# A rope block computed once: the product with the sine swaps the two halves of 64 rows

## The reference

```python
q_hk  = (hidden_q @ Wq.T).reshape(B, S, 16, 128)
q_big = jnp.einsum('bshk,hkq->bshq', q_hk, w_kc_q)      # 384 wide
q_big = q_big * cos + rotate_half(q_big) * sin          # rope over the 384
q_r   = jnp.einsum('bshq,hqr->bhsr', q_big, W_qr)       # 64 wide
# rotate_half(x) = concatenate([-x[..., 192:], x[..., :192]])
attn  = softmax(q_r . k_r);  ctx_c = attn @ kv_r
```

## Time and profile before

| what | value |
| --- | --- |
| runs of the kernel | 1120.31, 1122.6 and 1126.47 us, median 1122.6 us |
| the profiled execution | 1126.12 us |
| its span, first to last instruction | 1124.3 us |
| mean granted TensorE clock | 0.966 |
| PE busy in the span | 992.5 us, 88% |
| DVE busy | 693.1 us, 62% |
| ACT, POOL busy | 540.8 us, 513.3 us |

### The profile page before, as it was taken

One profiled execution on the slowest core, in us unless ns is written; L12 is line 12 of the kernel. 1 busy time (PEld: TensorE's weight loads), 2 busy tenths in 40 slices (PEclk: granted clock), 3 DMA queues, 4 the chain that ended last, 5 costly groups with the idle time before them and its releaser, 6 DMA issues. The chain is left out here.

```text
span 1124.3 us, 19812 instructions
## 1 busy us (share of the span) xinstructions
PE 992.5 (88%) x6202; PEld 578.6 (51%) x6202; DVE 693.1 (62%) x1187; ACT 540.8 (48%) x1224; POOL 513.3 (46%) x646
## 2 busy tenths in 40 slices
PE   0679999999999999899658569999999988998998
PEld 0335555555555555444223235777777764444543
DVE  2768778787878777396678534766666663323112
ACT  1345656565655656200376415777777773105400
POOL 2956766667666766100133205666666671110000
PEclk9999999999999999999888869999999999998999
DMA  7111121303122101341300002222222003204001
GB/s 219 43 57 58 51 66 42 89 28 89 31 86 65 42 19 30 140 160 65 112 1 29 20 19 67 66 66 65 65 65 65 0 1 143 73 1 159 0 29 38
DMA packets 24191, 69.23 MB, mean 62 GB/s; under 512 B 3162, under 2 KB 5338, under 8 KB 21719
## 3 DMA queue, kind: packets, MB, share of 16 engines
q1 hardware_dynamic: 18656, 58.01, 15.4%
q10 hardware_dynamic: 5492, 10.67, 3.6%
HBM read 64.99 MB, written 3.67 MB: 61 GB/s over the span
## 5 line engine op out<-in xcount | busy, mean ns | idle before, releaser
L1077 POOL TENSOR_SCALAR scratch<-scratch,rinv 112x375 f32<-112x375 f32 x256 | 155.4, 620 | 148.8 <-DVE rinv L944 148.8
L819 ACT ACTIVATE scratch<-ps,mxn 112x375 f32<-112x375 f32 x256 | 144.1, 571 | 59.0 <-DVE mxn L939 58.9
L1194 PE MATMUL ps<-arena 128*128 128x512 f16 x672 | 149.5, 385 | 2.3 <-PEq L600 2.3
L939 DVE TENSOR_REDUCE mxn<-ps 112x2 f32<-112x750 f32 x128 | 119.5, 933 | 41.7 <-PE ps L633 41.7
L1059 POOL TENSOR_TENSOR scratch<-scratch 128x896 f32<-128x896 f32 x64 | 104.5, 1633 | 60.1 <-DVE scratch L963 59.6
L684 PE MATMUL ps<-xnT,scratch 128*128 128x448 f16 x576 | 125.1, 364 | 3.8 <-DVE scratch L1014 2.4
L671 PE MATMUL ps<-scratch,kvn_hi 125*128 125x224 f16 x768 | 119.9, 260 | 4.4 <-DVE scratch L985 2.3
L656 PEld LDWEIGHTS ps<-ident,scratch 112*125 112x125 f32 x768 | 100.0, 188 | 42.4 <-issue 35.3
L1069 POOL TENSOR_TENSOR scratch<-scratch 128x375 f16<-128x375 f32 x128 | 115.3, 901 | 10.9
L656 PE MATMUL ps<-ident,scratch 112*125 112x112 f32 x768 | 106.5, 275 | 10.9 <-DVE scratch L1005 9.1
L829 ACT ACTIVATE scratch<-ps 125x672 f16<-125x672 f32 x128 | 94.2, 736 | 43.5 <-PE ps L656 42.5
(11 more groups left out here) (137 smaller groups left out, 1440.0 us busy)
## 6 DMA issues: line engine op xcount, KB each, us to landing
scratch<-in_wq SPq DMA_DIRECT2D x16, 512.0 KB, 5.0
scratch<-in_wo SPq DMA_DIRECT2D x16, 512.0 KB, 3.6
wabs<-in_w ACTq DMA_DIRECT2D x32, 256.0 KB, 3.0
scratch<-in_w SPq DMA_DIRECT2D x8, 1024.0 KB, 4.8
scratch<-in_W SPq DMA_DIRECT2D x8, 1024.0 KB, 6.4
scratch<-in_kcq SPq DMA_DIRECT2D x8, 512.0 KB, 5.5
scratch<-in_qr SPq DMA_DIRECT2D x32, 128.0 KB, 3.8
scratch<-in_kcq SPq DMA_DIRECT2D x8, 384.0 KB, 3.5
```

Of the source, the lines that this page charges most:

```text
L819: last = nc.scalar.activation(prob[0:S, s % 2, hh, :], scores_ps[0:S, hh, 0:L], ACT.Exp, bias=mxn[0:S, s % 2, hh:hh + 1], accum_out=rsum[0 ...
L939: nc.vector.tensor_reduce(mxn[0:S, s % 2, :], scores_ps[0:S, :, 0:L], AX_X, ALU.max, negate=True).then_inc(max_done, 1)
L1077: last = nc.gpsimd.tensor_scalar(prob[0:S, s % 2, hh, :], prob[0:S, s % 2, hh, :], rinv[0:S, s % 2, hh:hh + 1], P_SCALE, ALU.mult, ALU.mult)
L1194: last = nc.tensor.matmul(ps[:, b, :], a[:, h, ds(t * P, P)], c[:, h, :], start=(h == 0 and i == 0), stop=(h == H - 1 and i == 2))
```

## The change

The fourth block is gone: (B, u, 3) is taken out of all lists, and the split of the weight takes 2 x 384 of its 2 x 512 elements. The product of block 2 with the sine is made from the bank of block 2 by two operations of 64 rows each: one reads rows 64 to 127 and writes rows 0 to 63, the other the other way round. The sine table of block 2 is loaded with its halves exchanged, so that bank and table are read at the same rows; its load is three transfers in place of one. The second addition on POOL and the reuse of roped and turned wait for (B, u, 2) in place of (B, u, 3). The banks are dealt out again over 38 groups in place of 42.

```diff
-    [TURN, SCORES, ("A", 3), ("S", 1), ("K", 3), *ropes(2, 2, 3)],
-    [TURN, SCORES, *ropes(3, 0, 1), ("S", 2), ("K", 4), *ropes(3, 2, 3)],
+    [TURN, SCORES, ("A", 3), ("S", 1), ("K", 3), *ropes(2, 2)],
+    [TURN, SCORES, *ropes(3, 0, 1), ("S", 2), ("K", 4), *ropes(3, 2)],
...
-        kcq_hi, a = view(scratch, a, [2, 512], F16)
-        kcq_lo, a = view(scratch, a, [2, 512], F16)
+        kcq_hi, a = view(scratch, a, [2, DCQ], F16)
+        kcq_lo, a = view(scratch, a, [2, DCQ], F16)
...
-            act.dma_start(ropeq[:, :, :], tab["ropeq"]).then_inc(s_ropeq, 16)
+            act.dma_start(ropeq[:, 0:5, :], tab["ropeq"][:, 0:5, :]).then_inc(s_ropeq, 16)
+            act.dma_start(ropeq[0:R, 5, :], tab["ropeq"][R:P, 5, :]).then_inc(s_ropeq, 16)
+            act.dma_start(ropeq[R:P, 5, :], tab["ropeq"][0:R, 5, :]).then_inc(s_ropeq, 16)
...
-                        for dst, t in (((roped[:, u % 2, 0], 0), (turned[:, 1], 4)),
-                                       ((roped[:, u % 2, 1], 1), (turned[:, 0], 3)),
-                                       ((roped[:, u % 2, 2], 2),),
-                                       ((turned[:, 2], 5),))[j]:
+                        low, high, every = slice(0, R), slice(R, P), slice(0, P)
+                        for dst, t, rows, to in (
+                                ((roped[:, u % 2, 0], 0, every, every), (turned[:, 1], 4, every, every)),
+                                ((roped[:, u % 2, 1], 1, every, every), (turned[:, 0], 3, every, every)),
+                                ((roped[:, u % 2, 2], 2, every, every), (turned[:, 2], 5, high, low),
+                                 (turned[:, 2], 5, low, high)))[j]:
+                            n_rows = rows.stop - rows.start
                             last = nc.vector.tensor_tensor(
-                                dst.rearrange("p (b n) -> p b n", b=B // 2), src,
-                                ropeq[:, t:t + 1, :].to_broadcast([P, B // 2, S]), ALU.mult)
+                                dst[to].rearrange("p (b n) -> p b n", b=B // 2), src[rows],
+                                ropeq[rows, t:t + 1, :].to_broadcast([n_rows, B // 2, S]),
+                                ALU.mult)
...
-                        pool.wait_ge(group_out, nth_group(q, ("B", u, 3 if second else 1)))
+                        pool.wait_ge(group_out, nth_group(q, ("B", u, 2 if second else 1)))
```

More of the change, by code:

```diff
@@ L70 @@
     [TURN, SCORES, ("A", 2), ("S", 0), ("K", 2), *ropes(2, 0, 1)],
-    [TURN, SCORES, ("A", 3), ("S", 1), ("K", 3), *ropes(2, 2, 3)],
-    [TURN, SCORES, *ropes(3, 0, 1), ("S", 2), ("K", 4), *ropes(3, 2, 3)],
+    [TURN, SCORES, ("A", 3), ("S", 1), ("K", 3), *ropes(2, 2)],
+    [TURN, SCORES, *ropes(3, 0, 1), ("S", 2), ("K", 4), *ropes(3, 2)],
     [TURN, SCORES, ("S", 3), ("K", 5), ("C", 1), ("U", 0)],
     [TURN, SCORES, ("A", 0), ("G", 0), ("S", 4), ("K", 6), *ropes(0, 0, 1)],
-    [TURN, SCORES, ("A", 1), ("S", 5), ("K", 7), ("R", 0), *ropes(0, 2, 3)],
-    [TURN, SCORES, *ropes(1, 0, 1), ("S", 6), ("K", 0), *ropes(1, 2, 3)],
+    [TURN, SCORES, ("A", 1), ("S", 5), ("K", 7), ("R", 0), *ropes(0, 2)],
+    [TURN, SCORES, *ropes(1, 0, 1), ("S", 6), ("K", 0), *ropes(1, 2)],
     [TURN, SCORES, ("S", 7), ("K", 1), ("C", 0), ("U", 1)],
@@ L110 @@
     [SCORES, TURN, NORM, ("A", 2), ("S", 0), *ropes(2, 0, 1)],
-    [SCORES, TURN, NORM, ("A", 3), ("S", 1), *ropes(2, 2, 3)],
-    [SCORES, *ropes(3, 0, 1), TURN, ("S", 2), *ropes(3, 2, 3), NORM],
+    [SCORES, TURN, NORM, ("A", 3), ("S", 1), *ropes(2, 2)],
+    [SCORES, *ropes(3, 0, 1), TURN, ("S", 2), *ropes(3, 2), NORM],
     [SCORES, TURN, ("S", 3), NORM, ("L", 0), ("C", 1), ("U", 0)],
     [("L", 1), SCORES, TURN, NORM, ("A", 0), ("G", 0), ("S", 4), *ropes(0, 0, 1)],
-    [SCORES, TURN, NORM, ("A", 1), ("S", 5), ("R", 0), *ropes(0, 2, 3)],
-    [SCORES, *ropes(1, 0, 1), TURN, ("S", 6), *ropes(1, 2, 3), NORM],
+    [SCORES, TURN, NORM, ("A", 1), ("S", 5), ("R", 0), *ropes(0, 2)],
+    [SCORES, *ropes(1, 0, 1), TURN, ("S", 6), *ropes(1, 2), NORM],
     [SCORES, TURN, ("S", 7), NORM, ("C", 0), ("U", 1)],
@@ L130 @@
     [NORM, ("K", 2), *ropes(2, 1)],
-    [NORM, ("K", 3), *ropes(2, 3)],
-    [*ropes(3, 1, 3), NORM, ("K", 4)],
+    [NORM, ("K", 3), *ropes(2, 2)],
+    [*ropes(3, 1, 2), NORM, ("K", 4)],
     [NORM, ("K", 5)],
     [NORM, ("K", 6), *ropes(0, 1)],
-    [NORM, ("K", 7), *ropes(0, 3)],
-    [*ropes(1, 1, 3), NORM, ("K", 0)],
+    [NORM, ("K", 7), *ropes(0, 2)],
+    [*ropes(1, 1, 2), NORM, ("K", 0)],
     [NORM, ("K", 1)],
@@ L422, in start_vector @@
             nc.vector.tensor_copy(identb[:, :], eye)
-            dve.wait_ge(s_ropeq, 16)
+            dve.wait_ge(s_ropeq, 48)
         def start_tensor(pe):
@@ L869, in weights_high @@
                         if not (isinstance(q, int) and q == 0):
-                            act.wait_ge(group_done, nth_group(q - 1, (("A", 3), ("B", 3, 3))[n]))
+                            act.wait_ge(group_done, nth_group(q - 1, (("A", 3), ("B", 3, 2))[n]))
                         if n == 0:
@@ L874, in weights_high @@
                         else:
-                            dst, src = kcq_hi.rearrange("p c n -> p (c n)"), raw_kcq
+                            dst = kcq_hi
+                            src = raw_kcq.rearrange("p (h n) -> p h n", h=2)[:, :, 0:DCQ]
                         nc.scalar.activation(dst, src, ACT.Copy,
@@ L996, in group_lo @@
                         if kind == "B":
-                            if g[2] in (0, 3) and not (first(p) and n == 0):
-                                dve.wait_ge(rope_add, nth(q, 8, 2 * (n - 1) + g[2] // 3))
+                            if g[2] in (0, 2) and not (first(p) and n == 0):
+                                dve.wait_ge(rope_add, nth(q, 8, 2 * (n - 1) + g[2] // 2))
                             rope(p, q, g).then_inc(group_out, 1)
@@ L1012, in weights_low @@
                         dve.wait_ge(split_hi, nth(q, 2, n))
[L1013 to L1017, removed]
+                        hi, lo, src = ((wq_hi, wq_lo, raw_wq.rearrange("p (c n) -> p c n", c=DK)),
+                                       (kcq_hi, kcq_lo, raw_kcq.rearrange(
+                                           "p (h n) -> p h n", h=2)[:, :, 0:DCQ]))[n]
+                        nc.vector.scalar_tensor_tensor(lo, src, W_SCALE, hi, ALU.mult,
+                                                       ALU.subtract).then_inc(split_lo, 1)
                     def iteration(p, slots=range(B)):
@@ L1088, in iteration @@
                                 elif g[0] == "B" and runs(p, g):
-                                    add(pair_of(p, g), g[1], g[2] == 3)
+                                    add(pair_of(p, g), g[1], g[2] == 2)
                                 elif g[0] == "K" and runs(p, g):
```

## The result

The changed kernel takes 1133.78 us (median of 4 runs, 1133.01 to 1137.87), the kernel before 1122.92 us (4 runs). The ratio is 1.0102, interval 1.0065 to 1.0139: slower, by 10.9 us. The prediction had 1130 us and a range of 1119 to 1135.5. The profiled execution of after took 1133.01 us, with a span of 1131.1 us.

A forecast was written before the change was run, and what follows sets the result against it. DVE's rope string and POOL's additions ahead of C1 and C0 bound the pair, not PE's work. +4.8 (C1) + 4.6 (C0) - 2.4 (split) + 0.6 (prologue) + 0.1 (start) = +7.7 us: 1130 us, range 1119 to 1135.5.

The forecast's parts named there:

- the forecast's own range: Total time if the forecast's mechanism holds, with held starts and the split at their bounds: 1124.6 to 1133.6 us.
- the full range: Total time with rivals 1 (products overlap, 1121.5 us) and 3 taken in: 1119 to 1135.5 us.
- rival 3: Split of w_kc_q meets POOL's operation at its beginning, waits 0.9 us not 0.56, gain gone: 1133.2 us; chance 0.14.
- What bounds the kernel: Steady pair of 49.96 us: C1 and C0 hang on DVE's string and POOL's additions; PE's saving becomes waits.
- the sign to look for: In the profile after, PE's gap stands ahead of C1 and C0, released by POOL's addition.
- No overlap: DVE's block 2 rope: operations that change first row don't overlap, 0.65 us each instead of 0.53, 1.96 for three.
- the overlapping case: DVE's block 2 rope with full overlap: 0.53 us each, three in 1.61 us up to the next start.
- C1, +0.60 forecast: Rope of (B,2,2) to C1: longer DVE string delays POOL's second addition, C1 0.60 us later, eight times: +4.8 us.
- shift of (B,2,2)'s rope: Start of (B,2,2)'s rope moving against (B,2,0); claimed unchanged, a move would mean the prediction is wrong.
- C0, +0.66 forecast: Rope of (B,0,2) to C0: same steps as for C1, 0.66 us later, seven times: +4.6 us.
- The split: Split of w_kc_q on DVE, behind C1: 768 elements for 1024, gain 0.35 us a pair, seven times: -2.4 us.
- Prologue and start: Before the steady pairs: first C0 later by 0.6 us, sine table's three transfers 0.1 us.

The follow-up runs named there:

- e3: The changed kernel with block 2's sine product as one operation of 128 rows, the exchange left out; 1113.0 us, ratio 0.9908 to the kernel before.
- e4: The changed kernel, but C waits for POOL's second addition of its last head only ahead of its last four matmuls (block 2); 1124.7 us, ratio 1.0007.
- e5: e4 with DVE's low half of the transposes put between two ropes in slots 2 and 6 instead of behind both; 1111.6 us, ratio 0.9898.
- e1: The changed kernel with both 64-row sine products reading and writing rows 0 to 63, that of rows 64 to 127 left out; 1128.2 us, one run.
- e10: The changed kernel with its two exchanged 64-row products in the other order, same result; 1135.5 us, one run.
- e6: The kernel before, all four blocks kept, with the edits of e4 and e5; 1128.4 us, ratio 1.0046.
- e9: The changed kernel, but the split of w_kc_q takes all 2 x 512 elements again; 1134.6 us, one run.
- e2: The changed kernel without the exchange: each 64-row product reads and writes its own half of the rows; 1135.0 us, one run.
- e8: e5 with C going head by head instead of block by block, each head waiting for its own additions; 1122.2 us, ratio 0.9991.
- e7: e5 with POOL making keys 4 and 0 ahead of the normalisation of slots 2 and 6; 1119.5 us, ratio 0.9971.

## Why the prediction was right

The mechanism was right and its price was too low: +7.7 us forecast, +10.9 measured. The 1133.8 us lie 0.2 above the forecast's own range (1124.6 to 1133.6); the full range holds them because it took in rival 3, more than half of which came true.

- **What bounds the kernel.** Shown by e3 and e4: the pair hangs on DVE's string and POOL's addition ahead of C. PE's 0.57 us a group became waits (1.18 us at the transposes, 0.3 to 0.4 at C). The prediction named only the wait at C, as the sign to look for. The larger part stands at the transposes, behind DVE's low half, and holds PE once C's wait is cut: e5, which moves the low half forward, gains another 1.22 us a pair over e4.
- **No overlap.** The choice between 0.53 and 0.65 us for one product was right; no row of the kernel before decided it, and e1 and e10 do: 1.93 us from the first rope to the maximum, 1.96 forecast. e1 gives the overlapping case, 1.60. A held operation starts 0.02 us behind the end of the one before, not 0.04.
- **C1, +0.60 forecast.** C0 to C1 grew by 0.67 us. From the rope to C1 it is 9.20 less 8.62, +0.58; 0.08 came ahead of the rope, from (B,2,0) on (6.94 in place of 6.86 us). That is the shift of (B,2,2)'s rope which the prediction had named as a sign of being wrong; it is small, but it was not forecast. The rope starts 0.85 us behind its first matmul, 0.77 before. Why stays open.
- **C0, +0.66 forecast.** From the rope to C0 it is +0.55 us. The string up to the rope's end took 7.85 us where 7.92 were forecast, and C0 came 1.26 us behind that end, not 1.30.
- **The split: the term that was mis-sized.** Forecast -0.35 us, measured -0.11. The run fell by 0.27, but the wait for POOL grew from 0.56 to 0.72; the prediction had counted on it to fall. That is 0.24 us more than forecast, of the 0.41 us a pair by which rival 3 (gain gone) lies above the forecast. C1 to C0 grew by 0.46 us, 0.31 forecast: 0.24 more from the split, 0.11 less from the term before, and 0.02 in the rest. The pair so grew by 1.13 us, 0.91 forecast. Over seven pairs the split alone is 1.7 us.
- **Prologue and start.** Forecast +0.7. From x's load to the first C0 it is 39.68 us after and 39.71 before, but two things cancel there. From the rope of (B,0,2) to C0 it is 8.51 us after and 7.88 before, +0.63, as forecast. The rope came 0.66 us sooner, and that is chance: the first 12 matmuls of A took 3.98 us after and 4.64 before, 3.94 in e6, which does the same as before there, and 2.43 to 4.64 us over all profiles. The queue had 160 packets more, not 128; a cost of the added transfers doesn't show.
- **The first pair.** It was priced like the rest and grew by 0.90 and 0.85 us, where a later pair grew by 0.67 and 0.46. Part of it is the clock: 0.83 granted in 80 to 100 us, 0.50 from 86 to 90, which is the lower of the two levels, and 1.00 before. There the six transposes took 1.57 us in place of 0.88 and C1 2.96 in place of 2.48. PE had stood idle 1.38 us for the rope of (B,3,0) and 1.18 for the low half ahead of it.

From x's load to the last C1 the profiles differ by 427.30 - 418.24 = 9.1 us, and to the end of the span by 7.5; behind the first attention, where nothing was changed, 1.5 us come back. The medians differ by 10.9 us, the interval holds 7.3 to 15.6. The chance of the prologue hides 0.7 of the 3.4 us between the profiles' 7.5 and the medians' 10.9. Where the rest lies stays open: the runs of each kernel spread over 5 to 6 us, and stretches at a lower clock, as in the long pairs of e9 and e10, may be among it; no run shows that.

## What to carry to other kernels

Work that is taken off the busiest engine is gained only if no string through other engines is as long; go through one period and write down by how much each wait could have come sooner, and for whom. Two half-height operations cost two whole ones on DVE (622 and 617 ns each), and more where they change rows. When a string through DVE and POOL ends at PE, look at what PE truly needs first: waiting for the last addition only at the matmul that reads it, and putting the result that PE waits for ahead of one that it doesn't, turned this change from 1.0% slower into 1.0% faster (e5, 1111.6 us).

## What the runs showed of the hardware

- A DVE operation that starts at another row than the last one of its kind (input from PSUM, input from SBUF, output) starts 0.02 us behind its predecessor's end instead of 0.08 us ahead of it: 0.10 to 0.12 us each, with starts at rows 0 and 64. The operation that pays may stand behind one that doesn't touch that memory (e2, e10).
- DVE's float32 split from SBUF to SBUF and POOL's operations shut each other out. With 768 elements it ended 0.81 us behind the operation that POOL was in: it took 1.00 us with 0.19 of that left (e4), 1.24 with 0.44 (e5) and 1.53 with 0.72 (after). POOL's next one took 1.48 or 1.75 us in place of 0.90. The Trainium skill has this as an exclusive lock ("SBUF — State Buffer", section "SBUF: two separate sides"); the trace agrees.
- C's matmuls write 64 rows of the bank each. Written to the two halves in turn, 12 take 2.48 us; six to one half and then six to the other take 3.28 us (e8), though the work is the same. No run here shows why.
- The same 12 matmuls of A at the start of the loop took between 2.43 us (e9) and 4.64 us (before, e2, e7), at a granted clock of 1.00 in all four.
